# A fused graph layer on one core: the first projected tile goes through four of six weight blocks ahead of a wait, and the first expert's rows are fetched part by part

## What is computed

```python
x = x + gnn(xn, edge_index, W, b) + mix(xn, w_qkv, b_qkv, w_proj, b_proj)   # xn = layernorm(x)

# mix, for each of 12 heads of 64 features
A = q @ k.T
numerator = 1.0 + A + 0.5 * A * A
attn = numerator / numerator.sum(axis=-1, keepdims=True)
out = (attn @ v, heads side by side) @ w_proj + b_proj

# ffn on xf = layernorm(x): E = 8 experts, capacity 195, inner width 384
routes, prob_max = argmax and max of softmax(xf @ switch_w + switch_b)
rank = place among the tokens of the same expert, by falling prob_max
buf[e, rank] = xf                                  # where rank < capacity
h = gelu(buf @ w1 + b1, approximate=False)
o = h @ w2 + b2
y = where(kept, o[routes, rank], xf) * prob_max
x = x + y
```

## Time and profile before

| what | value |
|---|---|
| three runs | 1017.2, 1019.64, 1021.0 us; median 1019.64 |
| the profiled execution | 1020.73 us, its span 1019.0 us |
| busy: TensorE, VectorE, ScalarE, POOL | 89%, 75%, 48%, 35% of the span |
| mean granted clock of TensorE | 0.948 of full speed |
| chain that ended last, by engine | PE 55%, DVE 18%, issue 11%, DMA 7%, ACT 5% |
| one row fetch (line 1810), 16 of them | 1.015 / 1.034 / 4.463 us on POOL (least, median, most) |

### The profile page before, as it was taken

The page is one execution under the profiler, slowest core; times in us unless marked ns, Lnnn a source line. Parts: engine busy times, 40 slices in busy tenths (PEclk is TensorE's granted clock), DMA queues, the critical chain, the costliest instruction groups (busy, mean ns, idle before and its releaser), DMA issues.

```text
span 1019.0 us, 15414 instructions
## 1 busy us (share of the span) xinstructions
PE 906.3 (89%) x5154; PEld 859.9 (84%) x5154; DVE 760.4 (75%) x1570; ACT 488.4 (48%) x720; POOL 359.7 (35%) x236
## 2 busy tenths in 40 slices
PE   2899789989989989999999899979999995499895
PEld 2899689989989989988988789969999995398884
DVE  6778459989989989989988798554666666567773
ACT  2221256766766766767667641340323222255540
POOL 1014455545445554654555620000000001526562
PEclk9899799999999999999999899998999995599998
DMA  9986462364464364355436379255676634767861
GB/s 275 353 146 176 93 123 32 65 114 81 63 114 81 60 113 78 59 110 83 66 44 146 57 118 207 60 147 129 186 204 183 168 122 132 213 200 239 273 203 47
DMA packets 137614, 136.70 MB, mean 134 GB/s; under 512 B 70561, under 2 KB 118276, under 8 KB 136545
## 3 DMA queue, kind: packets, MB, share of 16 engines
q1 hardware_dynamic: 109646, 119.29, 44.9%
q0 software_dynamic: 27520, 16.67, 11.7%
q10 hardware_dynamic: 403, 0.17, 0.1%
HBM read 94.31 MB, written 38.17 MB: 130 GB/s over the span
## 4 chain that ended last, share of the span: by engine, by line
PE 55%; DVE 18%; issue 11%; DMA 7%; ACT 5%; POOL 1%; SPq 1%; DVEq 0%; ACTq 0%; POOLq 0%
PE ps L2027 9%; PE ps L2028 9%; PE ps L2029 9%; PE ps L1202 7%; PE ps L1186 4%; PE ps L1187 4%; PE ps L1623 3%; DMA out<-oE,ids 3%; DVE Pl L1061 3%; PE ps L1624 3%; DVE Ph L1059 2%; ACT Ph L852 2%; DMA Cs<-counts 2%; PE ps L1162 1%; ACT Pf L874 1%
## 5 line engine op out<-in xcount | busy, mean ns | idle before, releaser
L388 POOL DMA_INDIRECT counts<-countc,idxu x157 | 274.3, 1747 | 258.6 <-DMA counts<-countc,idxu 222.5
L1061 DVE SCALAR_TENSOR_TENSOR Pl<-Pf,Ph 125x832 fp32r<-125x832 f32 (+1 forms) x180 | 184.2, 1027 | 44.0 <-ACT Ph L852 40.4
L874 ACT ACTIVATE Pf<-ps 125x832 f32<-125x832 f32 (+1 forms) x180 | 156.0, 867 | 127.2 <-PE ps L1187 119.1
L1202 PE MATMUL ps<-Ph,vsb 125*128 125x416 f32 (+1 forms) x360 | 133.4, 371 | 23.2 <-DVE Pl L1061 23.0
L1202 PE MATMUL ps<-Pl,vsb 125*128 125x416 f32 (+1 forms) x360 | 127.9, 355 | 0.0
L1202 PEld LDWEIGHTS ps<-Ph,vsb 125*128 125x128 f32 x360 | 68.6, 191 | 39.1 <-DVE Pl L1061 26.0
L2027 PE MATMUL ps<-wH,XH 128*125 128x384 f32 x240 | 84.5, 352 | 4.1 <-DVE wL L481 4.1
L2027 PE MATMUL ps<-XH,wqkH 128*128 128x416 f32 (+1 forms) x216 | 83.1, 385 | 4.4 <-DVE wqkL L299 2.4
L2028 PE MATMUL ps<-wL,XH 128*125 128x384 f32 x240 | 82.9, 346 | 0.0
L2029 PE MATMUL ps<-wH,XL 128*125 128x384 f32 x240 | 82.6, 344 | 0.0
L852 ACT ACTIVATE Ph<-Pf 125x832 fp32r<-125x832 f32 (+1 forms) x90 | 80.5, 895 | 0.8
(11 more groups left out here) (281 smaller groups left out, 2196.2 us busy)
## 6 DMA issues: line engine op xcount, KB each, us to landing
Cs<-counts SPq DMA_DIRECT2D x17, 546.9 KB
w1s<-L_ffn_w SPq DMA_DIRECT2D x8, 1152.0 KB, 6.4
w2s<-L_ffn_w SPq DMA_DIRECT2D x8, 1152.0 KB
odram<-OHL SPq DMA_DIRECT2D x12, 625.0 KB, 8.4
oS<-odram SPq DMA_DIRECT2D x10, 750.0 KB, 4.8
vdram<-VS SPq DMA_DIRECT2D x10, 672.0 KB
vsb<-vdram SPq DMA_DIRECT2D x12, 560.0 KB
kt<-keyd SPq DMA_DIRECT2D x5, 1280.0 KB
```

The lines of the kernel that those rows point to most:

```text
L388: pool.indirect_dma_start(out=counts, out_offset=bass.IndirectOffsetOnAxis(ap=idxu[:, c:c + 1], axis=0), in_=countc[:, c:c + 1], in_offset ...
L874: act.activation(Pf[:, i % RING, :, 0:w], ps[0:T, 2 * (i % 2):2 * (i % 2) + 2, 0:w], ACT.Square, bias=1.0).then_inc(sq_done, 1)
L1061: dve.scalar_tensor_tensor(out=p, in0=f, scalar=1.0, in1=h.bitcast(F32), op0=ALU.add, op1=ALU.subtract).then_inc(p_lo, 1)
L1202: ins = pe.matmul(ps[:, 4 + s % 2, 0:w], vsb[:, 2 * kp + t, a, :], part[:, m % RING, t, 0:w], start=(kp == 0 and t == 0 and part is Ph), s ...
```

## The change

For tile 0 the projection is split: both halves go through blocks 0 to 3 behind w_lo 8, then both through blocks 4 and 5 behind w_lo 9. For expert 0 each part's fetch waits for its own copy of the numbers (ids_done 1, then 2), behind its fetches POOL adds one to consts, and VectorE waits for that sixth count before its two plain operations.

```diff
--- before.py
+++ after.py
@@ -1571,6 +1571,7 @@
                 dve.tensor_copy(pmc[0:n, :, t:t + 1].rearrange("p e o -> p (e o)"), ps[0:n, 2 * t, E:2 * E]
                                 ).then_inc(ids_done, 1)
             dve.wait_ge(xf_done, NT)
+            dve.wait_ge(consts, 6)
             plain(NT - 2)
             plain(NT - 1)
             steps_before.append(order.n)
@@ -1701,15 +1702,17 @@
                 if i >= 1:
                     transposes(i - 1)
                 pe.wait_ge(os_in, 16 * i + 16)
-                if i == 0:
-                    pe.wait_ge(w_lo, 9)
-                else:
+                if i >= 1:
                     pe.wait_ge(x1_done, i)
-                for c in range(2):
-                    if c == 1 and i >= 2:
-                        pe.wait_ge(pm_evac, i - 1)
-                    ins = product(pe, ps[0:T, 4 + c, 0:HALF], lambda k: (oS[:, k, 0, :], oS[:, k, 1, :]),
-                                  lambda k: (wpH[:, k, c * HALF:(c + 1) * HALF], wL3[:, k, c * HALF:(c + 1) * HALF]), KT)
+                for k0, k1_ in ([(0, 4), (4, KT)] if i == 0 else [(0, KT)]):
+                    if i == 0:
+                        pe.wait_ge(w_lo, 8 if k0 == 0 else 9)
+                    for c in range(2):
+                        if c == 1 and i >= 2:
+                            pe.wait_ge(pm_evac, i - 1)
+                        ins = product(pe, ps[0:T, 4 + c, 0:HALF], lambda k: (oS[:, k, 0, :], oS[:, k, 1, :]),
+                                      lambda k: (wpH[:, k, c * HALF:(c + 1) * HALF], wL3[:, k, c * HALF:(c + 1) * HALF]),
+                                      KT, k0, k1_)
                 ins.then_inc(pj_mm, 1)
                 if i >= 1:
                     logits(i - 1)
@@ -1807,6 +1810,8 @@
 
             def fetch_rows(e):
                 for t, (r0, n) in enumerate(CTILES):
+                    if e == 0:
+                        pool.wait_ge(ids_done, t + 1)
                     pool.indirect_dma_start(out=xe[0:n, e % 2, t, :], out_offset=None, in_=xfd,
                                             in_offset=bass.IndirectOffsetOnAxis(ap=ids[0:n, t, e:e + 1], axis=0),
                                             bounds_check=N - 1, oob_is_err=False).then_inc(xe_in[e % 2], 16)
@@ -1821,8 +1826,8 @@
 
             pool.wait_ge(consts, 5)
             pool.wait_ge(xf_store, MOVED * NT)
-            pool.wait_ge(ids_done, 2)
             fetch_rows(0)
+            pool.sem_inc(consts, 1)
             fetch_rows(1)
             pool.wait_ge(plain_store[0], MOVED * NT // 2)
             pool.wait_ge(plain_store[1], MOVED * NT // 2)
```

## The result

The changed kernel took 1006.5, 1006.57, 1007.04 and 1007.44 us, median 1006.8, against a before of 1018.4 (1011.7 to 1021.0): a ratio of 0.9884, with a 95% interval of 0.9839 to 0.9929. Over all comparisons 28 executions of the changed kernel have a mean of 1010.1 and 109 of the kernel before 1018.9 (standard errors 0.75 and 0.5; single executions above 1200 us left out), so the change is worth **8.8 us**, give or take 1.8 (two standard errors), and the first four executions were lucky by some 3 us. Without the executions that took over 1.5% more than the fastest of their kernel (27 and 93 are left) it is 7.9 us, give or take 1.5.

The account below looks back on a forecast made before the run. It took waits of TensorE as the bound where later work waits for TensorE, at the first projected tile and the first expert's rows. 5.9 + 1.0 = 6.9 us off the median of 1019.64 gave 1012.7, range 1007.5 to 1015.5.

Parts of the forecast that it names:

- Part one: First projected tile: 24 matmuls run ahead of the wait for wL's last piece; gain 5.9 us.
- The idle of 3.7 us: TensorE's idle between tile 0's gather and product, waiting for wL's last piece; 3.7 of the 5.9 us gain.
- The half clock: Tile 0's product: its first matmuls at the 1.2 GHz level behind the idle; 2.2 of the 5.9 us gain.
- rival 2: First projected tile: the clock falls in spite of the missing idle; gain 3.7 + 1.0 = 4.7, 1014.9 us; chance 0.10.
- place one: The first projected tile, where TensorE idled 3.54 us between gather and product and then ran at 1.2 GHz.
- Part two: First expert's rows: part-by-part fetch and VectorE's wait; gain 1.0 us, ends -0.7 and +3.4.
- the hold let go too soon: First expert's rows: POOL's step follows its fetch's issue, so VectorE starts 0.1 us ahead of part 1's fetch.
- part 1 is blocked again: First expert's rows: part 1's fetch waits through VectorE's plain operations and w1L, done at 875.1 against 875.7.
- Rival 1: First expert's rows: the hold works or POOL gets in between two operations; gain 5.3, 1008.4 us; chance 0.27.
- from the first product on everything moves as a whole: Behind the first expert's first product: the loop's fetches and loads are released by it, so its gain stays whole.
- The sum: Whole kernel: 5.9 + 1.0 = 6.9 us gained, median 1012.7 us; chance of the forecast 0.55.

Follow-up runs that it names:

- p1_only: The kernel before with only the first tile's product split, 24 matmuls over four blocks and 12 over two: ratio 0.9957.
- before_b: The kernel before, unedited, run once more for its trace: 1017.5 us.
- no_hold: The changed kernel without POOL's added step and VectorE's wait for it ahead of the plain operations: ratio 0.9956.
- both_held: The changed kernel with both parts fetched behind the second copy of row numbers, VectorE's wait kept: ratio 0.9958.

## Why the prediction was right and wrong

**Part one, 5.9 us: the mechanism was right, the term mis-sized.** It measured 2.5 us on average (standard error 1.4). The idle of 3.7 us was read from one execution in which wL's last piece came 3.55 us behind the gather; the median is 1.3. The half clock was put down to that idle alone. With the split there is no idle in any trace, yet 0 to 8 of the 36 matmuls run at the lower level (2 in the changed kernel's trace, 6 in p1_only). The gather has a gap of its own, for HH: in the five traces with slow matmuls it is 2.1 to 4.9 us, in the eleven without 0.95 to 1.74. So rival 2 was partly true, and 0.3 to 1.2 us go to it in those five.

**Behind place one: right.** From the second gather to the first copy of row numbers it takes 167.7 us in all 20 traces, within 0.04. Every us gained at place one arrives; nothing is late next.

**Part two, the hold let go too soon: right to 0.04 us.** POOL's step follows the issue; VectorE leads by 0.14 us, where 0.1 was predicted.

**Part two, 1.0 us: the step that failed** is "part 1 is blocked again: plain from 869.7 to 871.6, w1L to 874.1, the fetch done 0.97 behind it". The fetch is held only to the end of the first plain, its generation ends 6.35 us behind the first copy instead of 9.9, and its rows land ahead of w1s (TensorE turns them at 10.6, w1s is there at 18.9). I took the row of 4.46 us beside plain and w1L for a fetch that waits out everything VectorE has in its list. It was one that began 0.01 us ahead of the second plain and missed that boundary and the next. Rival 1, "POOL gets in between two operations", gave 5.3 us; 5.0 were measured at the first product in the first pair of profiles. By means of five traces of part two as it stands and three without it, it is 4.7 at the first product (16.1 and 20.8), 4.4 at the second expert's (32.6 and 37.0), and 4.0 at the end (149.3 and 153.3). So "from the first product on everything moves as a whole" is not quite right either: the rounding of the next expert's w1 moves by only some 2 us (18.9 to 19.7 against 20.8 to 21.5).

**The sum.** 2.5 and 4.0 are 6.5 us, by the means of few traces each; predicted were 6.9, of which 5.9 and 1.0. The times say 7.9 to 8.8, with an uncertainty of up to 1.8, and place one's mean is itself uncertain by 1.4; whether the 1.4 to 2.3 between them are real stays open. That the total came near is luck: one term was too large by 3.4 and the other too small by 3.0. That the first median fell outside the range is in part bad luck: the changed kernel's executions scatter from 1005.2 to 1022.8 us with a mean of 1010.1, which lies inside, and for the scatter of a median I had allowed 0.9.

## What to carry to other kernels

A cost read from one profile is one draw: before pricing a wait, ask whether what ends it is a DMA, and read it in a second execution. Where POOL's fetches share time with VectorE's wide two-operand operations, look at the distance from the fetch's start to VectorE's next boundary (here it decided for the row fetches, with another bound for the stores), and know that a small operation ahead of the wide ones can do the work of a semaphore. A fetch that is no longer held lands beside the next load, so find out what the brake had protected.

## What the runs showed of the hardware

- A row fetch of the first expert that VectorE holds is let in at a boundary between two of its operations and ends 0.89 to 0.98 us behind the end of the one that held it. The boundaries 0.01 and 0.17 us after the fetch's start were missed, those at 0.31, 0.45, 0.72, 0.80 and 0.85 were taken. A row fetch that missed one missed the next too (before, before_b, p1_only, no_hold).
- The stores of finished rows missed a boundary 0.51 to 0.64 us after their start, 97 times in 20 traces, and took 3.9 to 4.3 us.
- tensor_tensor alone holds a fetch: 3.32 us beside w1L.
- A semaphore step behind an indirect DMA in POOL's list let VectorE start 0.14 us before that DMA's generation began (changed kernel), and 1.02 us before it where the DMA stood in line behind another (both_held).
- TensorE's clock can be at the 1.2 GHz level in a stretch with no idle in it (679.0 to 682.2 in the changed kernel, 0.50), behind a gap of 2.71 us in front of it.
- The same program reaches the same point 13.6 us apart from execution to execution.
